# Decoder block on one core: the second projection of v put between the two halves of the second round's value products

## The reference

```python
x = x + attn(layernorm(x), Wq, Wk, Wv, lambda, g1, g2, g3, W1, W2)   # linear attention over 16 heads of 16, in each row
x = x + xattn(layernorm(x), ctx_512, ...)                            # one softmax attention over 256 context rows
x = x + ffn(layernorm(x), wi, wo, lora_A, lora_B, gate, ...)         # relu MLP 256-1024-256, 8 adapters, top 2
```

```python
Q, K, V = xn @ Wq.T, xn @ Wk.T, xn @ Wv.T        # each (rows, 16 heads, 16)
pQ, pK = elu(Q), elu(K)                          # halves 1 and 2 of the 16
w = Q1 @ (K1.T @ V) - lmb * Q2 @ (K2.T @ V)      # over the heads of one row
attn = rms(w) * g2 ; attn = rms(attn) * g3 + attn
out = gelu(attn @ W1.T) @ W2.T + attn
```

## Time and profile before

| | us |
|---|---|
| median of three runs | 655.89 |
| lowest, highest | 653.71, 657.14 |
| profiled execution, its own time | 654.88 |
| its span in the profile | 653.2 |
| TensorE busy (matmul) | 608.2 (93%) |
| VectorE busy | 477.2 (73%) |
| ScalarE busy | 386.2 (59%) |
| GpSimd busy | 372.5 (57%) |
| granted TensorE clock, mean | 0.989 of full speed |

### The profile page before, as it was taken

How to read it: one execution, slowest core, us unless ns; L and a number is a source line. 1 busy time by engine, 2 the same in 40 slices (tenths; PEclk the granted TensorE clock), 3 DMA queues, 4 the chain that set the end, 5 groups by cost and what they waited for, 6 DMA issues and landing times.

```text
span 653.2 us, 21459 instructions
## 1 busy us (share of the span) xinstructions
PE 608.2 (93%) x8338; PEld 570.8 (87%) x8338; DVE 477.2 (73%) x1133; ACT 386.2 (59%) x853; POOL 372.5 (57%) x404
## 2 busy tenths in 40 slices
PE   2887999999989899789999999999999999999997
PEld 2666887777788798789999999999999999999997
DVE  8786488786656888878778686677777777777672
ACT  3573557776766776556768467474456456455432
POOL 5221198898677797894645445545545545643333
PEclk9899899998999999999999999999999999999999
DMA  9653344354466442220212201101101101100000
GB/s 236 176 127 100 77 108 129 82 148 104 114 178 189 156 153 66 74 89 17 91 42 82 74 17 57 42 18 42 41 3 41 40 0 40 40 16 1 17 18 34
DMA packets 79719, 50.27 MB, mean 77 GB/s; under 512 B 23048, under 2 KB 79632, under 8 KB 79632
## 3 DMA queue, kind: packets, MB, share of 16 engines
q1 hardware_dynamic: 79632, 49.07, 26.8%
HBM read 23.88 MB, written 12.58 MB: 56 GB/s over the span
## 4 chain that ended last, share of the span: by engine, by line
PE 66%; DVE 10%; issue 9%; ACT 5%; SPq 4%; POOL 4%; DMA 1%; POOLq 0%; DVEq 0%; ACTq 0%
PE banks L726 52%; PE banks L848 4%; PE banks L779 4%; PE banks L866 2%; POOL f_hT_lo L2087 2%; PE banks L884 2%; SPq L593 2%; ACT L1287 1%; SPq L578 1%; DVE p_xn L1602 1%; DMA attn_scratch<-h_wn 1%; DVE m_hT_lo L1656 1%; DVE h_sm L1645 1%; ACT m_g L1287 1%; DVE f_hs L1827 1%
## 5 line engine op out<-in xcount | busy, mean ns | idle before, releaser
L2087 POOL TENSOR_TENSOR f_hT_lo<-f_hs,f_hT_hi 128x512 fp32r<-128x512 f32 x64 | 87.4, 1366 | 112.9 <-ACT f_hT_hi L1400 112.8
L2103 POOL TENSOR_TENSOR h_rh<-h_ms,mhalf 128x16 f32<-128x16 f32 x32 | 94.2, 2953 | 0.4
L1827 DVE SCALAR_TENSOR_TENSOR f_hs<-banks,nbic,f_h 128x256 f32<-128x256 f32 x128 | 54.6, 478 | 47.4 <-PE banks L726 47.4
L726 PE MATMUL banks<-woT_hi,f_hT_lo 128*128 128x256 f32 x256 | 74.5, 291 | 0.3 <-POOL f_hT_lo L2087 0.3
L726 PE MATMUL banks<-f_adT_hi,lbT_lo 128*128 128x256 f32 x256 | 73.0, 285 | 0.6 <-DVE f_adT_lo L1815 0.6
L726 PE MATMUL banks<-f_adT_hi,lbT_hi 128*128 128x256 f32 x256 | 71.7, 280 | 0.0
L726 PE MATMUL banks<-f_xT_hi,wiT_lo 128*128 128x256 f32 x256 | 71.7, 280 | 0.0
L726 PE MATMUL banks<-f_adT_lo,lbT_hi 128*128 128x256 f32 x256 | 71.6, 280 | 0.0
L726 PE MATMUL banks<-f_xT_lo,wiT_hi 128*128 128x256 f32 x256 | 71.5, 279 | 0.0
L726 PE MATMUL banks<-f_xT_hi,wiT_hi 128*128 128x256 f32 x256 | 71.5, 279 | 0.0
L726 PE MATMUL banks<-woT_hi,f_hT_hi 128*128 128x256 f32 x256 | 71.1, 278 | 0.0
(11 more groups left out here) (268 smaller groups left out, 1974.4 us busy)
## 6 DMA issues: line engine op xcount, KB each, us to landing
h_qk<-p_qk SPq DMA_DIRECT2D x64, 128.0 KB, 2.8
xin<-in_x_dram SPq DMA_DIRECT2D x16, 256.0 KB, 3.1
h_v<-p_v SPq DMA_DIRECT2D x128, 32.0 KB
attn_scratch<-h_wn SPq DMA_DIRECT2D x16, 256.0 KB, 2.7
m_w<-attn_scratch SPq DMA_DIRECT2D x16, 256.0 KB, 3.7
m_x<-in_x_dram SPq DMA_DIRECT2D x16, 256.0 KB, 3.0
x_scratch<-m_y SPq DMA_DIRECT2D x16, 256.0 KB, 2.6
c_x<-x_scratch SPq DMA_DIRECT2D x16, 256.0 KB, 2.7
```

The lines of the kernel that those rows point to most:

```text
L726: ins = pe.matmul(acc, left(a), right(b), start=first and n == 0, stop=last and n == 2, skip_group_check=skip)
L1827: ins = dve.scalar_tensor_tensor(out=f_hs[:, j % 2, c * T:(c + 1) * T], in0=bank[HB[j]][:, c * T:(c + 1) * T], scalar=nbic[:, f:f + 1], in ...
L2087: pool.tensor_tensor(lo, f_hs[:, j % 2], hi.bitcast(F32), ALU.subtract).then_inc(f_hlo, 1)
L2103: pool.tensor_tensor(h_rh[:, H * i:H * i + H], h_ms[:, H * i:H * i + H], mhalf[:, 0:H], ALU.pow).then_inc(h_rhd, 1)
```

## The change

`head_values(1)` of unit u emits `project_v(1)` of unit u + 2 between its groups 3 and 4, that is behind 64 of its 128 matmuls. It is taken out of its old place, in the loop behind `turn_x(0)` and in the tail behind values (1); only that of unit 1, in step 4, where no values (1) are made, stays where it was. The projection's wait for VectorE's mask of bank 3 goes with it. The other engines' programs are as they were.

```diff
@@ head_values @@
                     if r or u.has(1):
                         pe.wait_ge(h_wTd, nth(u, SETS * ROUNDS, SETS * r))
                     for g in range(GR):
+                        if r == 1 and g == GR // 2 and u.index + 2 < SU:
+                            project_v(1)(Unit(0, u.index + 2, u.index + 2))
                         for c in range(SETS):
                             for i in range(ST):
                                 ins = pe.matmul(bank[4 + c][32 * i:32 * i + HD, g * HT:(g + 1) * HT],
@@ the order of TensorE @@
-                          (3, but(1, project_v(0))), (3, but(1, project(3))), (5, head_values(1)), (2, turn_x(0)), (3, project_v(1)),
+                          (3, but(1, project_v(0))), (3, but(1, project(3))), (5, head_values(1)), (2, turn_x(0)), (3, only(1, project_v(1))),
                           (2, turn_x(1)), (5, head_turn(0)), (4, head_values(0)), (5, head_turn(1)), (5, head_turn(2)),
...
             go(5, head_values(1))
-            go(7, project_v(1))
             go(5, head_turn(0))
```

## The result

The changed kernel takes **657.32 us**, the median of 20 runs (650.05 to 660.68), the kernel before on the same chip 654.18 us, also 20 runs (650.86 to 657.14). The ratio is **1.0037**, with a 95% interval of 1.0019 to 1.0054: +2.4 us, between +1.2 and +3.5. The profiled execution takes 657.43 us, its span 655.7, mean granted clock 0.987 (before 654.88, 653.2, 0.989).

What follows compares the result with a forecast made beforehand. TensorE was taken to bound the kernel, except 157 to 181 us, where the chain runs through SyncE. The terms 0.6 + 0.5 + 0 + 0 + 1.4 gave +2.5 us, 658.4 against the median 655.89, range 654.3 to 661.8.

Steps and rivals of the forecast that it cites:

- Step 5 and 6, +0.6 and +0.5: Between values (1) and head_turn(0): head_turn(0) starts later, behind ScalarE's copies that lost cover; +0.6 and +0.5 us.
- The switches: Two more switches between small tiles and full array around the moved projection; about 0.1 us, ends 0 and 0.2.
- Step 7, 0: The 0.63 us gap in values (1) goes, the later one in values (0) takes it back; 0 us.
- the case "there in time": In values (0), the late instruction block arrives before it is needed, so the step ends 0.9 us sooner.
- rival (b): Faster: late-instruction gaps go (1.4 us), a clock drop may be spared (1.7); 652.8 us; or the clock drops elsewhere; chance 0.09.
- Step 8, 0: Projection waits 0.4 us for bank 3's mask, but TensorE's 0.90 us standstill for h_wn absorbs it; 0, other end 0.95.
- Step 9 and the tail, +1.4: SyncE issues h_v later behind values (1), delaying the chain until 181 us; +1.4, beside TensorE's own 1.2, not added.
- The premise, "comes out at the end almost whole": TensorE is saturated from 400 us, so delay between 60 and 183 us reaches the end unless another engine sets the pace.
- (a): Instruction blocks come 5.3 us behind their boundary everywhere, opening gaps in values (0) of odd steps; +5.1, 663.5 us; chance 0.20.
- (c): Slack of ScalarE and SyncE eats the 0.6 and 0.5, early transfers catch the 1.4; no change, 655.9 us; chance 0.18.

Runs made afterwards that it cites:

- e9: Changed kernel with value products ordered by bank, the projection between the banks and ScalarE's copy of bank 4 released early; 659.48 us, 1.0087 to the kernel before.
- e3: Against the kernel before: three of the projection's six products in the middle of values (1), three behind turn_x(0); 655.45 us, 0.9991.
- e6: Changed kernel with SyncE's first four h_v transfers put behind its h_qk transfers of k; 657.65 us, 1.0058 to the kernel before.
- e1: Against the kernel before: projection whole behind values (1), ahead of turn_x(0), values not split; 655.51 us, 1.0013.
- e2: Changed kernel with the projection ahead of all 128 products of values (1), unsplit; 667.11 us, 1.0167 to the kernel before.
- e4: Against the kernel before: only unit 7's projection, in the tail, moved into values (1); loop as before; 654.96 us, 0.9989.
- e8: Against the kernel before: projection whole behind both turn_x, straight ahead of head_turn(0), in the loop; 654.85 us, 1.0004.
- e5: Changed kernel with only the loop's projections (units 2 to 6) moved, the tail's left behind values (1); 657.25 us, 1.0049 to the kernel before.
- e11: Changed kernel with VectorE making the second round's copy of bank 5 in place of ScalarE; 657.50 us, 1.0046 to the kernel before.
- e7: Kernel before with SyncE's first four h_v transfers put behind its h_qk transfers of k, as a control; 656.28 us, 1.0028.
- e12: Kernel before with VectorE making the second round's copy of bank 5 in place of ScalarE, as a control; 655.91 us, 1.0029.
- e10: Kernel before with value products ordered by bank and bank 4's copy released early, projection in its old place; 655.65 us, 1.0016.

## Why the prediction came out as it did

The total is right: +2.5 us was forecast, +2.4 measured. The forecast held a change of under 0.5% for one that can't be told; the many runs behind the result do tell it, since the lower end of the interval lies above 1. The number is right in part by luck, because errors cancel: in the profiled execution the delay at the end of the heads is 5.0 us, twice the forecast, and half of it is lost on the way to the end. Of the 5.0, 1.5 are the clock of this one execution; the rest, 3.5, is still 1.0 more than the sum. Point by point:

**Step 5 and 6, +0.6 and +0.5: right as far as head_turn(0); what comes behind it was left out.** In step 5 head_turn(0) was forecast at 74.6 and came at 74.67, released by ScalarE's L1260 as forecast. In step 6 it came at 95.09, 1.46 us later than before where values (1) had come 0.96 later: +0.5. But the parts differ. The forecast wait of about 0.45 us is 0.16 by the profile, because TensorE's own way had grown too. And the delay grew behind it. Of the 1.05 us of step 5, the split and the projection between the halves made 0.30 (3.19 against 2.89), the transpositions of x 0.09 (0.93 in e9, where no wait follows them, against 0.84), what is left of the wait 0.3 (head_turn(0) could have started near 74.35), and values (0) 0.33. Two terms were off. The switches were put at 0.1, with 0.2 as the end; they measure 0.30, outside my bounds, in e3 too. I had drawn them from one pair of neighbours in the tail, 0.03 us, and that was the projection behind the products; a second half behind the projection stood nowhere in the trace. By the Trainium skill's rule that a change of tiling mode drains TensorE (TensorEngine Tiling (Array Packing), Tiling Modes, Key Properties) there was a price, and the trace agrees, though it doesn't tell the drain from slower products. The other, and the larger one, is values (0), a piece that the change doesn't touch and that I costed at nothing without saying so: 0.33 us in step 5 and 0.41 in step 6 (97.50 - 95.67 = 1.83 against 95.58 - 94.16 = 1.42). Its cause is open (e6, e1), and the kernel before has the same in step 9.

**Step 7, 0: wrong, near one of its ends.** I said that the first gap goes, and that the third takes it back. Both are gone, and from values (1) to head_turn(1) it is 121.17 - 114.32 = 6.85 us against 7.79 (110.43 to 118.22): -0.94, the 0.9 that I had as the case "there in time". That the gaps are instructions that came late was right (e2); that the block of the third gap would come at 117.64 or later was not. How much comes late changes between executions, though: e4's loop is that of the kernel before, and its trace has no such gap. So the 0.94 is what these two traces show, and not all of it need be the change. The half clock then took 1.5 us elsewhere in the step, as rival (b)'s last sentence allowed, and the traces of e8, which between 60 and 180 us has it in step 5 alone, and e3, in 7 and 9, show that where it falls changes from one execution to another.

**Step 8, 0: right.** From values (1) to the scores behind them pass 144.99 - 134.77 = 10.22 us, before 141.87 - 131.81 = 10.06. The projection waits for L1646 as forecast, 0.18 instead of 0.4, and the 0.90 for ScalarE's h_wn took up the rest, as I had reckoned. In step 7 it doesn't wait, against the forecast: the mask had ended at 113.53, and the projection starts at 115.11. The slow clock isn't the whole reason, for in e5, at full clock there, the mask ends at 113.85 and the projection starts at 114.00.

**Step 9 and the tail, +1.4: seen, but worth nothing at the end.** SyncE's first h_v of step 5 was forecast at 73.6, and in step 9 SyncE was to wait for the products. SyncE, changed kernel, timeline:

```profile
73.66 2.63 SPq L593 DMA_DIRECT2D h_v<-p_v  x4
...
161.87 2.69 SPq L593 DMA_DIRECT2D h_v<-p_v  x4
```

and its waits between 157 and 163 us:

```profile
SPq L470 <- PE banks L868: 1.7, 1, 1.7
```

It waits in step 9 as forecast, and issues 4.6 us later than in rows 2, as the products end 4.8 later. From step 9 to the scores behind the tail the delay grows by 1.9 us, of which 1.2 is the wait of head_turn(0). But e4 has that wait and is as fast as before, and e5 lacks the move in the tail and is as slow as the whole change. The term was right as a local delay and wrong as a part of the sum: of its 1.4 us nothing that can be told reaches the end.

**The premise, "comes out at the end almost whole": half wrong.** From 400 us on TensorE is saturated as rows 1 say. But between 183 and 208 us there is slack, and 2.7 of 5.0 us went there. I had read the part from 400 on and the part to 183, and taken what lies between for the first. From the start of values (1) in the tail to the end of the span pass 478.1 us before and 476.8 after, and in the experiments 475.9 (e2) to 479.7 (e4): a delay that is there by the tail comes out but for 1 or 2 us, and the 1.2 added behind it doesn't show. The traces in the usual order of products bear this out: between the scores behind the tail and the value products at 206 us, those with the move in the tail (changed kernel, e3, e4, e6, e11) make good 2.2 to 2.7 us of their delay, those without it (e1, e5, e7, e8, e12) 0.5 to 1.8.

**The rivals.** (a) fell with the gaps: there is none in values (0) of steps 5, 7 and 9. (b) saw both gaps go, 1.4 us together; what it missed is that the other terms weren't zero, and that the half clock of step 9 wasn't spared but came again, at 154 us. (c) is out by the interval, whose lower end is +1.2 us.

**What stays open.** In time, the split and the lost cover can't be set apart. e1 (no split, cover whole) and e3 (split, half the cover) cost nothing; e9 (split, cover restored by other means) costs more than the change itself, but with a product order of its own, in which 64 products take 1.03 us instead of 0.79. That the split costs where the cover is down to 0.8 us, and that the whole cover without a split or half the cover with one doesn't, is what the runs show; which of the two leads isn't settled. The 1.0 us per step is read from one execution of each kernel. Most agree: 19.4 to 19.5 us from step 5 to 6 in before, e1, e4, e8 and e12, 20.4 and 20.6 in the changed kernel and e5. But with SyncE's order changed it is 20.1 with the change (e6, whose values (0) are fast) and 20.7 without (e7, which has a gap of 1.0 us in its values (0)), so the step's length hangs on more than TensorE's order.

## What to carry to other kernels

Work that fills in behind a producer is also the cover under which its consumer copies; before moving it forward, compare what remains with the copy's duration, and if it doesn't reach, move half or leave it; here half cost nothing and gained nothing. Cost also the pieces behind the edit: one that isn't touched, values (0), made a third of step 5's loss. Large matmuls between runs of small ones also give the instruction supply its time: taken from between them they left 8.4 us of gaps (e2). So look where they stand in the stream, and not only at how many there are. Read the stretch between the edit and the saturated end by itself: a delay that is summed up to the last step of a loop may be worth half at the end.

## What the runs showed that was not expected

- TensorE's gaps without a releaser are late instructions: each of 121 ends 1.2 to 1.8 us after a packet of 16 KiB of the queue q8 (instruction) has landed. In the value products, 46 to 195 us, they add up to nothing to 0.6 us with the projection in the middle of values (1), nothing to 3.8 with it between the two runs, 8.4 with it ahead of them (longest 2.1 us). With the products bank by bank, which are slower, and the projection in its old place there are 0.2 us of them (e10).
- The same 128 products of values (0), at full clock, start in 1.27 to 1.35 us when undisturbed and in 1.67 to 1.71 in steps 5, 6, 7 and 9 of the changed kernel and in step 9 of the kernel before, with no waits between them; in the changed kernel's step 5 with little DMA traffic (0.17 of the engines).
- The order of the products matters by itself: alternating between the two banks, 64 of them take 0.79 us from start to next start; one bank after the other, 94.76 - 93.73 = 1.03 (e9).
